# TensorE's image loop: bands of images 1 to 7 written out, replaced by a loop over images with fourteen bands written out once

## The reference, cut to what matters

```
def reference(x, W_id, b_id, ..., W_enc, b_enc):
    xn = _gn(x)                                   # group norm, 32 groups, x is (8, 64, 224, 224)
    res = conv3x3(xn, W_id, b_id)                 # all eight images
    cA, cH, cV, cD = _swt2_level3(xn[0])          # wavelet bands of image 0 alone
    low_att = _attention(cA, ...); high_att = _attention([cH, cV, cD], ...)
    out = leaky_relu(conv3x3(concat([low_att, high_att]), W_enc, b_enc), 0.01)
    return x + out + res
```

## Time and profile before

| | us |
|---|---|
| median of the three runs (range) | 1970.77 (1967.54 to 1971.35) |
| the profiled execution, its own time | 1965.66 |
| its span, first to last instruction | 1963.7 |
| TensorE busy in it | 1934.4 |
| VectorE busy | 1464.4 |
| GpSimd busy | 1032.8 |
| ScalarE busy | 1008.3 |

### The profile page before, as it was taken

The page is one execution under the profiler, slowest core; times in us unless marked ns, Lnnn a source line. Parts: engine busy times, 40 slices in busy tenths (PEclk is TensorE's granted clock), DMA queues, the critical chain, the costliest instruction groups (busy, mean ns, idle before and its releaser), DMA issues.

```text
span 1963.7 us, 79515 instructions
## 1 busy us (share of the span) xinstructions
PE 1934.4 (99%) x35530; PEld 1609.5 (82%) x35530; DVE 1464.4 (75%) x2253; ACT 1008.3 (51%) x1067; POOL 1032.8 (53%) x775
## 2 busy tenths in 40 slices
PE   8999999999999999999999999999999999999998
PEld 7987999999999999668897888767877778766664
DVE  5665578778878876577777777777777777777776
ACT  4555666666666676634444344434444444444432
POOL 0005878887888885444444444444444444444444
PEclk9999999999999999999999999999999999999999
DMA  8883598888888884588888877887887878877774
GB/s 172 238 289 98 166 276 214 218 214 216 209 219 215 209 215 104 134 202 205 198 205 208 199 204 197 207 200 194 201 210 198 200 202 206 204 201 199 206 207 124
DMA packets 132647, 391.92 MB, mean 200 GB/s; under 512 B 49676, under 2 KB 50448, under 8 KB 118128
## 3 DMA queue, kind: packets, MB, share of 16 engines
q1 hardware_dynamic: 132336, 387.10, 77.2%
HBM read 258.56 MB, written 128.45 MB: 197 GB/s over the span
## 4 chain that ended last, share of the span: by engine, by line
PE 36%; issue 33%; POOL 26%; ACT 1%; DVE 1%; DMA 1%; POOLq 1%; SPq 0%; DVEq 0%; ACTq 0%
POOL stage L1689 26%; PE ps L1097 13%; PE ps L1063 7%; PE ps L621 5%; PE ps L1067 5%; PE ps L1066 3%; PE ps L623 3%; POOLq L1687 1%; DMA big<-in_x 1%; DVE pool_of L1284 0%; DVE pool_of L1272 0%; DMA pool_of<-in_x 0%; POOL pool_of L1358 0%; POOL pool_of L315 0%; POOL pool_of L306 0%
## 5 line engine op out<-in xcount | busy, mean ns | idle before, releaser
L1689 POOL TENSOR_TENSOR stage<-stage,big 128x448 f32<-128x448 f32 x448 | 511.5, 1142 | 642.7 <-DVE stage L1664 639.9
L1601 PE MATMUL ps<-pool_of,w_hi 64*64 64x448 f16 x12096 | 645.9, 350 | 3.7 <-issue 3.3
L1601 PEld LDWEIGHTS ps<-pool_of,w_hi 64*64 64x64 f16 x12096 | 450.4, 107 | 147.3 <-issue 8.7
L1601 PE MATMUL ps<-pool_of,w_lo 64*64 64x448 f16 x8064 | 452.4, 350 | 2.2 <-issue 2.2
L1601 PEld LDWEIGHTS ps<-pool_of,w_lo 64*64 64x64 f16 x8064 | 304.5, 107 | 98.3 <-issue 4.8
L1664 DVE SCALAR_TENSOR_TENSOR stage<-ps,w_max,pool_of 64x448 f32<-64x448 f32 x448 | 305.9, 683 | 45.7 <-PE ps L1601 33.0
L1284 DVE BATCH_NORM_STATS2 pool_of<-big 128x6 f32<-128x448 f32 x392 | 232.5, 617 | 76.8 <-DMA big<-in_x 76.6
L1515 ACT ACTIVATE pool_of<-pool_of 128x2240 f16<-128x2240 f32 x56 | 126.4, 2258 | 313.9 <-PE ps L1601 313.9
L1664 DVE SCALAR_TENSOR_TENSOR stage<-ps,w_max,xs 64x448 f32<-64x448 f32 x384 | 262.1, 683 | 33.5 <-PE ps L1601 22.1
L1515 ACT ACTIVATE pool_of<-xs,pool_of 128x2240 f16<-128x2240 f32 x48 | 108.4, 2258 | 284.4 <-PE ps L1601 284.4
L1601 PE MATMUL ps<-big,w_hi 64*64 64x448 f16 x4032 | 225.4, 350 | 0.0
(11 more groups left out here) (197 smaller groups left out, 2487.4 us busy)
## 6 DMA issues: line engine op xcount, KB each, us to landing
out<-stage SPq DMA_DIRECT2D x448, 224.0 KB, 3.2
big<-in_x SPq DMA_DIRECT2D x392, 224.0 KB, 5.2
pool_of<-in_x SPq DMA_DIRECT2D x104, 560.0 KB, 7.0
xs<-in_x SPq DMA_DIRECT2D x96, 560.0 KB, 7.1
pool_of<-row_filtered SPq DMA_DIRECT2D x110, 224.0 KB, 3.8
pool_of<-in_x SPq DMA_DIRECT2D x32, 392.0 KB, 7.4
row_filtered<-big SPq DMA_DIRECT2D x2, 6272.0 KB, 22.7
row_filtered<-big SPq DMA_DIRECT2D x4, 1568.0 KB, 8.9
```

The costliest lines, as they stand in the source:

```text
L1601: mm = pe.matmul(psum[4 * p + 2 * g + r][C * k:C * k + C, 0:NT], w[lanes, t, :], v[lanes, y:y + 2, kx:kx + W], start=(j == 0), stop=(j == ...
L1689: pool.tensor_tensor(stage[p][:, r, g, :], stage[p][:, r, g, :], e_map[:, e:e + NT], ALU.add)\
```

## The change

TensorE's part for images 1 to 7 becomes a loop on the engine. Bands 1 to 13 of image 0 stay written out, with constants. Behind them a register `freed` is set to 8 (2 x 14 - 1) = 216, and a `Fori` from 1 to 8 runs the fourteen bands with the number 14 i + b made from the loop's register. In the loop the waits for `hi_ready` and `lo_ready` are for counts worked out from that number, and the wait for `evac` is for `freed`, which goes up by 8 after each band. The wait for `pads_set`, which stood in band 0 alone, now stands in every band outside the loop. Band 0 goes through a new function `conv_first`. The matmuls, their order and their operands are the same.

```diff
@@ encoder, tensor
-            ahead.conv(pe, 0, 0)
+            ahead.conv_first(pe)
@@ main
-        def conv(pe, n, p):
-            if n == 0:
-                pe.wait_ge(pads_set, 4)
+        def conv(pe, n, p, freed=None):
             pe.wait_ge(hi_ready, n + 1)
             pe.wait_ge(lo_ready, n + 2)
-            pe.wait_ge(evac, 8 * (n + NB - 1))
+            if freed is None:
+                pe.wait_ge(pads_set, 4)
+                pe.wait_ge(evac, 8 * (n + NB - 1))
+            else:
+                pe.wait_ge(evac, freed)
+                pe.reg_add(freed, freed, 8)
...
+        def conv_first(pe):
+            conv(pe, 0, 0)
+
...
         def tensor(pe):
             pe.wait_ge(chain, 1)
-            for n in range(1, B * NB):
-                conv(pe, n, n % 2)
+            for b in range(1, NB):
+                conv(pe, b, b % 2)
+            freed = pe.alloc_register("freed")
+            pe.reg_mov(freed, 8 * (2 * NB - 1))
+            with pe.Fori(1, B) as i:
+                for b in range(NB):
+                    conv(pe, NB * i + b, b % 2, freed)
```

More of the change, by code:

```diff
@@ L77 @@
 Link = namedtuple("Link", "cleared einv_ready b32_in act_rows dve_rows first_split emx emax_part emax_all spread_max sx stat_in unit")
-Ahead = namedtuple("Ahead", "load dummies pads norms norm_first high full split edges root partners conv")
+Ahead = namedtuple("Ahead", "load dummies pads norms norm_first high full split edges root partners conv_first")
 def input_transform():
@@ L1692, in main @@
         ahead = Ahead(load=lambda sp, b: load(sp, 0, b), dummies=dummies, pads=pads, norms=norms, norm_first=first_norm,
-                      high=high, full=full, split=split, edges=edges, root=root_of, partners=partners, conv=conv)
+                      high=high, full=full, split=split, edges=edges, root=root_of, partners=partners, conv_first=conv_first)
         return Programs(sync, tensor, scalar, vector, gpsimd), ahead
```

## The result

| | before | after |
|---|---|---|
| median of four runs, us | 1969.15 (1965.66 to 1971.35) | 2018.38 (2017.41 to 2024.39) |
| ratio (95% interval) | | 1.0255 (1.0234 to 1.0276) |
| the execution whose rows stand here, its own time | 1965.66 | 2018.61 |
| its span | 1963.7 | 2016.4 |

The changed kernel is slower by 49.2 us by the medians, and by 52.95 us between the two profiled executions, against which the rows are summed. First the page after: the busy time, the instruction queue and TensorE's costliest form. Lines have moved, 1601 is now 1604, and 1526 is where it was.

A forecast was written before the change was run, and what follows sets the result against it. TensorE's own instruction stream was taken to bound the kernel. Back-branch idles of 37.2 us plus 10.2 us of clock made 47.4 us, giving 2013.1 for the profiled execution, 2018 us carried to the median; range 1982 to 2040.

The forecast's parts named there:

- Six idles at the seams, none elsewhere new: TensorE at the seams of images 1 to 7: six "issue" idles of 5 to 7 us, none between images 0 and 1.
- 6.2 us each, 37.2 in all: Loop's back branch, taken six times: TensorE idles while the head's block is fetched, 6.2 us each, 37.2 us.
- its ends of 2.0 and 7.6: Bounds in us on the idle per back branch, from the soonest and latest straight-code fetches examined.
- 1.45 us from landing to work: Delay between a code block's landing and TensorE resuming, 1.45 us, set against the sequencer's lead of 1.4 us.
- 1.7 us of clock each, 10.2 in all: TensorE behind each seam: clock falls after the idle, 1.7 us lost each, 10.2 us; ends 0 and 3.4 each.
- What stays: Other engines' code, q8's packets and the eight small idles remain: 0, ends a gain or loss of 7.2 us.
- "q8 keeps its packets": Instruction queue q8: as many blocks fetched as before, packets near 278 still.
- The block after the head: 0: Fetch of the block behind the loop's head hides under the head's block: 0, ends 0 and 2.3 us an edge.
- The registers: 0: Register instructions and waits per band, hidden by the sequencer's lead: 0, ends 0 and 12 us; binding rival 0.03.
- a free branch: Rival at the back branch: head's block already there, 0.05 us an edge, 1971 or down to 1964 us; chance 0.09.
- up to 7.2 us: Under the free-branch rival: the idles at block ends could vanish too, up to 7.2 us less, 1964 us; chance faster 0.03.

The follow-up runs named there:

- the hint: Changed kernel with a hint at the top of each pass of TensorE's loop naming the back branch and its target: 1975.91 us, ratio 1.0043.
- the heads at slot 200: Changed kernel with the loop's head put at slot 200 of its block of 256, instead of about 40: 2054.39 us in a single run.
- just ahead of a block's end: Changed kernel with the loop's seam moved to the middle of a band, last image written out, five taken branches: 2016.65 us, ratio 1.0247.
- the kernel without back branches: Changed kernel with images 1 to 7 written out, each in a loop that runs once, waits still against registers: 1966.55 us, ratio 0.9992.
- the pairs: Changed kernel with TensorE's loop over pairs of bands from band 2 of image 0 on, 55 passes: 1956.87 us, ratio 0.9924.
- a body of 3.4 blocks runs 48 times: Changed kernel with TensorE's loop over pairs of bands instead of images, 48 taken back branches: 1960.7 us in a single run.
- a body of twice that: Changed kernel with TensorE's loop over four bands, 24 passes, bands 14 and 15 written out: 2186.57 us in a single run.
- the kernel with five seams: Changed kernel with image 7 written out, five back branches at the head of band 0 instead of six: 2014.13 us, ratio 1.0227.
- the kernel with its seam in the middle of a band and the head at slot 8: Changed kernel with the seam in mid-band, five taken branches, and the loop's head at slot 8 of its block: 1992.17 us, ratio 1.0115.

## Why the prediction was right, and where it was off

The forecast of 2018 us met 2018.38, with its mechanism in each step, though two terms were small, and that the total still met the median is luck.

- *Six idles at the seams, none elsewhere new.* Right, all six on their place, and the hint shows that it is the branch's target that is missing.
- *6.2 us each, 37.2 in all.* Mis-sized: 41.9 us, 7.0 each, within its ends of 2.0 and 7.6. From the branch at 1236.7 to the landing at 1243.6 are 6.9 us where I took 6.2. And the step "1.45 us from landing to work" was short: the branch ends 1.4 us after the landing, and the first matmul comes 0.5 us later still, 1.85 in all. When the fetch is asked for is not in any row; the branch's start stands in for it.
- *1.7 us of clock each, 10.2 in all.* Mis-sized as well: 1.5 to 2.4 us, 12.4 for six. That idles of one us cost none was argued from the page's slices, which cannot show it: 1.7 us lost in a slice of 49 is still 0.9 or more. The stretch of 73.47 us behind the idle of 1.09 does show it, with a clock of 1.00.
- *What stays.* The other nine idles for "issue" are 6.0 us (18.6 less 6.88 and 5.67) against 5.5 and the 1.7 us of clock behind the one of 1.99 us did not recur. 41.9 + 12.4 + 0.5 - 1.7 = 53.1 us, against 52.95 between the profiled executions, and my 47.4 for the same was 5.6 us short. Between the medians there are only 49.2, as the profiled execution of before was the fastest of its four. I laid the sum on the median of the times shown, 1970.77, which was 5.1 us above that execution and 1.6 above the median of all four, 1969.15. So a sum 1.8 us short of the difference between the medians stood on a base 1.6 us too high, and the two errors cancelled. "q8 keeps its packets" missed eight, about one for each seam and two more.
- *The block after the head: 0.* Right for this loop, whose head lies well inside its block, and right that it is a matter of place: the heads at slot 200 and just ahead of a block's end have the second idle, of 0.2 to 1.3 us (2.6 at the loop's entry) and of 3.3 to 3.7.
- *The registers: 0.* Right, by the kernel without back branches.
- *The other side, a free branch.* The argument against it held for a body of 24 blocks. What I had not asked is how small a body must be: at 3.4 blocks it is free, and the block ends' gain of "up to 7.2 us" that I put under this rival is what the pairs bring: 7.5 us between the profiled executions. Between the medians it is 14.4, as the kernel before ran slower beside the pairs, 1971.26 us.

The Trainium skill, "Runtime: NRT & Kernel Launch", section "Instruction fetch mechanics", had the stall on a taken branch outside the present window, and the trace now agrees, with 8.2 us of branch. Its window of two pages does not: a body of 3.4 blocks runs 48 times with branches of 0.21 us. The measurement decides. Four or five blocks are held, and seven or eight, with the next one fetched ahead, are not.

## What to carry to other kernels

Read the instruction queue beside the data: where an engine's stream is the bound, each block of 256 instructions is a fetch that stands in line with the loads, and an idle for "issue" at equal counts of instructions is its sign. At a branch the idle can bear another engine's name; the row of the branch itself tells. Make a hot loop either small enough that its code stays (two bands here, some 873 instructions, 0.8% faster than straight code) or straight; a body of twice that was the worst here, as some 9 us are paid at every pass. If a large body must loop, hint the branch, and look where in the DMA's rhythm its last block begins and how far the head is from a block's end. In the last pass, whose branch is not taken, the hint cost an idle of 4.7 us here.

## What the runs showed of the hardware that I had not expected

- How late a fetch comes goes with the data transfers at its asking: the same branch takes 6.8 to 8.6 us at the head of a band and 3.8 to 5.1 in its middle, with q1 at 89.6% of the engines behind the one and 34.7% behind the other (5.2 us at one head of a band in the kernel with five seams). No kernel changed the loads alone.
- Straight code was not free on TensorE: 6.1 us in 1000, some 5 of them at block ends, with a wider spread between runs (11 us against 3).
- An idle of 1.99 us dropped the clock in the kernel before, and the 45 matmuls behind it took 4.14 us. One of 2.00 us at the same place did not in the pairs, where the same 45 take 2.46 us. In the kernel with its seam in the middle of a band and the head at slot 8, the clock stayed up behind an idle of 3.37 us and fell behind one of 3.18 (the second and the third seam). So an idle's length alone does not tell whether the clock falls.

```profile
808.45 2.46 PE L1604 MATMUL ps<-pool_of,w_hi 64*64 64x448 f16 x45 [2.00 <-issue]
```

```profile
1245.00:1250.00 5.00, 5.00 (x108) 3.81 (x112) 1.26 (x2) 0.00 (x0) 2.22 (x2) 1.00 0.97 257
1393.70:1398.70 5.00, 4.98 (x72) 3.01 (x76) 1.49 (x3) 0.00 (x0) 2.27 (x2) 0.67 0.98 256
```
